# A fused attention and mixture-of-experts block: weight splits spread over two slots, one operation moved, and the last wait moved from GpSimd to SyncE

## The chip, the core and the metric

The program runs on one core of one Trainium2 chip. TensorE (PE in the profile, PEld for its weight loads), VectorE (DVE), ScalarE (ACT), GpSimd (POOL) and SyncE (SP) each run their own stream of instructions, in the order in which the program wrote it, and wait for each other on semaphores. The metric is the device time of one execution in microseconds, lower is better; the figure compared is the median of several runs.

## The reference

For 1024 tokens of 512 numbers the reference computes a layer norm and adds three things: the input, a grouped-query attention and a mixture of experts.

```
xn  = layernorm(x)                                  # (4, 256, 512)
q   = xn @ Wq ; k, v = split(xn @ Wkv)              # 32 heads of 16, 8 groups, causal, per sequence of 256
att = softmax(mask(q k') / 4) v @ Wo + bo
scores = sigmoid(xn @ gate_w') + bias               # 16 experts, the best 4 of each token
ffn = sum over chosen e of cw[e] * (silu(xn Wg[e]') * (xn Wu[e]')) @ Wd[e]'   +  a shared expert of the same form
out = x + att + ffn
```

## The kernel before

**Slots.** The token rows that choose an expert are gathered in groups of 128, called slots. There are 47 slots (NSLOT), sorted by expert, so an expert's slots stand next to each other. Which slot begins a new expert depends on the data; here, read from where the weight splits stand in the trace, these are the slots 1, 6, 11, 12, 13, 18, 19, 20, 21, 22, 26, 29, 30, 32 and 40 (the first expert's slot 0 is prepared earlier).

**Steps.** The main part of the program, from about 112 us to 480 us, is 48 steps, 12 for each of the 4 sequences (`b`). Step s does slot s of the experts, and beside it a part of the attention: the 8 head groups `g` of a sequence are spread over its 12 steps j by a table, so that a group has one or two steps.

```
BESIDE = ((0, 1), (2,), (3,), (4, 5), (6,), (7, 8), (9,), (10, 11))
```

In step s TensorE transposes the rows of slot s+1 (L1265), multiplies slot s by the gate and up weights (`slot_gate_up`, 12 matmuls on L1209 with `xgT`), transposes the gated values of slot s-1 (L1232), multiplies slot s-2 by the down weights (`slot_down`, 6 matmuls on L1209 with `zT`), and does the attention's scores for the maxima (`scores_for_max`, L1244 and L1249, which overwrite the banks that the exponential reads), the scores (L1331 to L1339) and the weighted sum (`weighted`, L1354). In two steps of a sequence it also multiplies by the output matrix (`project_out`, L1366).

**Split weights.** The products of the experts are made three times, with a high and a low part of each operand. When a slot begins a new expert, its weights are split: ScalarE copies the high part (`weights_high`, L632), then VectorE subtracts it from the raw weights to get the low part (`gu_low`, L1012, for gate and up; `down_low`, L1047, for down). The gate/up weights come in two halves of 1024 columns (HALVES), the down weights in one. The raw weights (`wraw`) and the split ones (`wsplit`) have two places each, used by experts in turn. SyncE loads raw weights in one fixed order; the load of expert e waits until both halves of expert e-2 are split (L379), and ScalarE waits for the load at L631.

In step s both halves of slot s+1's weights are split: on ScalarE between `x_high` (L628, the high part of the rows) and `tanh` (L609), on VectorE between `x_low` (L1007) and `gated` (L842, L847). `slot_gate_up` of the next step waits for both. The splits stand in an If on a register that is 0 when the slot begins no new expert.

**What stands behind the splits.** On ScalarE a step ends with `z_rows` (L622, L624), `y_evac` (L658, the result of `slot_down`), `context_evac` (L715, first step of a sequence), `high16` (L711, the 16-bit high part of the exponentials) and the down split; the next step of a new group begins with the exponential (`numerators`, L705). On VectorE the step has `x_low`, `context` (L1071, L1072, L1076: the weighted sums divided by their denominators), the splits, `maxima` (L997, twice), `gated`, `z_rest` (L989), the down split, `attention_out` (L1086) and `low16` (L1065, which needs `high16`). In the first step of a group of two, `context` is left to the second, where it stands ahead of the splits and of `gated`. TensorE's `weighted` of one group waits for `context` of the group before (its sums, `csum_done`).

**End.** GpSimd gathers rows, adds each slot's result into the output by an indirect DMA (L506), and adds the attention's rows by a DMA (L513). After its last issue it waits for `att_out`, that is until the last of these has landed (L541), and then leaves its stream. SyncE has nothing to do after the last weight load. All engines meet in the barrier that ends the block (L93).

## Time and profile before

| what | value |
|---|---|
| median of 3 runs | 502.7 us (502.25 to 503.31) |
| profiled execution, its own time | 504.71 us |
| its span, first to last instruction | 502.9 us |
| PE busy | 454.6 us, 90% of the span |
| VectorE busy | 360.7 us, 72% |
| ScalarE busy | 284.4 us, 57% |
| GpSimd busy | 192.5 us, 38% |

Busy times are sums over the span; an engine that is 90% busy sets the pace in most stages, but what a change is worth is read from the waits of the stage that it touches.

### The profile page before, as it was taken

To read this page: it belongs to the slowest core of one execution; us is meant where nothing else is said; L and a number is where in the kernel's file an instruction comes from. 1 tells how busy PE (TensorE), PEld (TensorE's weight loads), DVE (VectorE), ACT (ScalarE), POOL (GpSimd) and SP (SyncE) were. 2 spreads that over 40 slices of the span, in tenths; PEclk is the share of its full clock that TensorE was granted. 3 is DMA by queue.
4 is the path that set the end of the run, shared out by engine and by line. 5 is a ranking of instruction groups with operands and counts; after the bars stand their busy time and mean duration, and the time that the engine had idled before them with its cause. 6 is when DMAs were issued, how large, how long until landed. Compare 5 with 4: busy or idle time off the path is not lost.

```text
span 502.9 us, 9687 instructions
## 1 busy us (share of the span) xinstructions
PE 454.6 (90%) x3074; PEld 348.6 (69%) x3074; DVE 360.7 (72%) x624; ACT 284.4 (57%) x435; POOL 192.5 (38%) x159
## 2 busy tenths in 40 slices
PE   5997999967998998999897999998999999999870
PEld 5776888845786786767675776686777857777630
DVE  7588874776787779849889887389789638775610
ACT  2732332504766776837787756486866637676510
POOL 2111649512444453324344444242344433353221
PEclk9998999988999998999999999998999999999995
DMA  6925853849947545886597778658864434443333
GB/s 254 410 64 144 182 197 90 290 158 216 273 119 174 121 73 145 227 266 117 92 293 201 246 184 139 193 116 180 239 133 87 85 66 73 76 85 46 49 55 42
DMA packets 31877, 77.92 MB, mean 155 GB/s; under 512 B 4048, under 2 KB 11728, under 8 KB 28912
## 3 DMA queue, kind: packets, MB, share of 16 engines
q0 software_dynamic: 11856, 27.27, 29.4%
q1 hardware_dynamic: 18864, 45.92, 28.7%
q10 hardware_dynamic: 1104, 4.06, 4.0%
q8 instruction: 28, 0.46, 0.4%
q14 instruction: 25, 0.20, 0.1%
HBM read 54.04 MB, written 23.07 MB: 153 GB/s over the span
## 4 chain that ended last, share of the span: by engine, by line
PE 59%; DMA 16%; DVE 10%; issue 5%; ACT 5%; ACTq 1%; DVEq 1%; POOL 1%; SPq 0%; POOLq 0%
PE psum L1209 34%; DMA out<-ysb,tab 8%; DMA out<-third_out,tab 4%; PE psum L1366 3%; PE psum L1172 3%; PE psum L1244 3%; PE psum L1354 3%; DMA xn_rows<-xn 2%; PE psum L1265 2%; PE psum L1249 2%; PE psum L1331 2%; PE psum L1232 2%; DVE wsplit L1012 2%; ACT wsplit L632 2%; DVE negm L997 1%
## 5 line engine op out<-in xcount | busy, mean ns | idle before, releaser
L1209 PE MATMUL psum<-wsplit,xgT 128*128 (+1 forms) x660 | 173.8, 415 | 11.1 <-DVE wsplit L1012 11.0
L1209 PEld LDWEIGHTS psum<-wsplit,xgT 128*128 128x128 f32 x660 | 126.0, 197 | 38.2 <-issue 12.9
L506 POOL DMA_INDIRECT out<-ysb,tab x32 | 55.5, 1734 | 127.1 <-ACT ysb L658 56.9
L1209 PE MATMUL psum<-wsplit,zT 128*128 (+1 forms) x330 | 92.7, 417 | 3.7 <-DVE zT L983 3.5
L1209 PEld LDWEIGHTS psum<-wsplit,zT 128*128 128x128 f32 x330 | 59.7, 192 | 16.8 <-issue 6.1
L997 DVE TENSOR_REDUCE negm<-psum 128x4 f32<-128x512 f32 x64 | 59.4, 954 | 12.6 <-PE psum L1249 12.2
L1065 DVE TENSOR_TENSOR plo<-xn,phi 128x1536 f16<-128x1536 f32 x32 | 56.2, 1756 | 11.1 <-ACT phi L711 10.1
L705 ACT ACTIVATE xn<-psum 128x1536 f32<-128x1536 f32 x32 | 46.3, 1448 | 22.4 <-PE psum L1339 14.0
L1007 DVE TENSOR_TENSOR xgT<-psum,xgT 128x512 fp32r<-128x512 f32 x47 | 32.3, 688 | 36.8 <-ACT xgT L628 36.0
L632 ACT ACTIVATE wsplit<-wraw (+1 forms) x48 | 48.9, 1054 | 5.8 <-SPq L376 5.8
L496 POOL DMA_INDIRECT xg<-xn_rows,tab x32 | 38.7, 1211 | 34.7 <-PE psum L1265 19.0
L506 POOL DMA_INDIRECT out<-third_out,tab x15 | 27.9, 1858 | 59.2 <-ACT third_out L658 24.9
L609 ACT ACTIVATE th<-psum 128x256 f32<-128x256 f32 x55 | 21.1, 384 | 46.2 <-PE psum L1209 46.0
L711 ACT ACTIVATE phi<-xn 128x1536 f16<-128x1536 f32 x32 | 47.2, 1475 | 0.0
L1012 DVE TENSOR_TENSOR wsplit<-wraw,wsplit (+1 forms) x32 | 37.8, 1221 | 7.7 <-ACT wsplit L632 5.5
L658 ACT ACTIVATE ysb<-psum,tab 128x512 f32<-128x512 f32 x32 | 21.9, 684 | 24.8 <-PE psum L1209 23.0
L628 ACT ACTIVATE xgT<-psum 128x512 fp32r<-128x512 f32 x47 | 27.9, 593 | 8.1 <-issue 8.1
L842 DVE SCALAR_TENSOR_TENSOR zh<-th,psum 128x256 f32<-128x256 f32 x55 | 22.8, 414 | 10.6 <-ACT th L609 7.9
L1366 PE MATMUL psum<-wo_sb,stage 128*128 128x512 f32 x64 | 28.9, 596 | 0.4 <-DVE xn L1086 0.4
L1172 PE MATMUL psum<-xT,wqk_sb 128*128 128x256 f32 x128 | 29.0, 380 | 0.0
L1354 PEld LDWEIGHTS psum<-v_pack,phi 128*128 128x128 f16 x384 | 20.8, 96 | 10.2 <-issue 7.8
L1172 PEld LDWEIGHTS psum<-xT,wqk_sb 128*128 128x128 f32 x128 | 24.2, 190 | 3.9 <-issue 0.5
(192 smaller groups left out, 728.4 us busy)
## 6 DMA issues: line engine op xcount, KB each, us to landing
wraw<-wexp SPq DMA_DIRECT2D x17, 1024.0 KB, 6.8
wraw<-wexp SPq DMA_DIRECT2D x17, 512.0 KB, 4.5
q_parts<-stage SPq DMA_DIRECT2D x16, 192.0 KB
xn<-x SPq DMA_DIRECT2D x4, 512.0 KB, 5.3
xn_rows<-xn SPq DMA_DIRECT2D x8, 256.0 KB, 9.7
ctxs<-x SPq DMA_DIRECT2D x8, 256.0 KB, 4.7
out<-ysb SPq DMA_DIRECT2D x8, 256.0 KB, 3.3
out<-xn POOLq DMA_DIRECT2D x8, 256.0 KB, 4.2
```

The lines of the kernel that those rows point to most:

```text
L496: nc.gpsimd.indirect_dma_start(out=rows_in[s % 3], out_offset=None, in_=xn_rows, in_offset=rows_of(s)).then_inc(xg_in[s % 3], 16)
L506: nc.gpsimd.indirect_dma_start(out=out, out_offset=rows_of(s), in_=rows_out[s % 3], in_offset=None, compute_op=ALU.add).then_inc(y_out[par ...
L632: S(wsplit[:, place, 0, cols], wraw[:, place, cols], ACT.Copy).then_inc(w_high[part], 1)
L705: S(pexp[:, g % 2, :], psum[:, 0:3, :].rearrange("p a n -> p (a n)"), ACT.Exp, scale=SCALE).then_inc(exp_done, 1)
L711: S(phi[:, g % 2, :], pexp[:, g % 2, :], ACT.Copy).then_inc(hi16_done, 1)
L997: V.tensor_reduce(negm[:, g // 4, 0, REP * (g % 4):REP * (g % 4) + REP, qt], s_, AX.X, ALU.max, negate=True).then_inc(negm_done, 1)
L1012: V.tensor_tensor(wsplit[:, place, 1, HALVES[half]], wraw[:, place, HALVES[half]], wsplit[:, place, 0, HALVES[half]].bitcast(F32), ALU.sub ...
L1065: V.tensor_tensor(plo[:, g % 2, :], pexp[:, g % 2, :], phi[:, g % 2, :], ALU.subtract).then_inc(lo16_done, 1)
L1172: last = MM(psum[:, dst, i * T:(i + 1) * T], wqk_sb[:, k, f * P:(f + 1) * P], xT[:, k, T * b:T * (b + 1)], start=k == 0, stop=k == KD - 1, ...
L1209: last = MM(dst, lhs(a, k), split_weights(place, w, c), start=m == 0, stop=m == len(products) - 1)
L1354: last = MM(psum[:, PV, c:c + VCOL], p_[:, g % 2, col:col + P], v_pack[:, QT * (g % B) + kt, 2 * b + g // B, 0:VCOL], start=m == 0, stop=m ...
L1366: last = MM(bank(to), ctxT[:, qt, k, :], wo_sb[:, k, :], start=k == 0, stop=k == KD - 1)
```

## The change

Three edits. First, the gate/up split of a new expert is cut in two: in step s the first half for slot s+2 and the second half for slot s+1. The first half stands, on ScalarE, behind `y_evac` and ahead of the second `context_evac` and of `high16`, and on VectorE at the very end of the step. Ahead of step 0, the first half for slot 1 is split. Second, the `context` that stood behind `x_low` now stands behind `gated`. Third, GpSimd's last wait is gone, and SyncE waits at its end for all result DMAs.

```diff
@@ sync
             announce(1, NE - 1)
+            for par in range(2):
+                newest = NSLOT - 1 - (NSLOT - 1 - par) % 2
+                sp.wait_ge(y_out[par], 16 + 16 * (newest // 2 + 1))
+            sp.wait_ge(att_out, 16 * QT * B + 16)
@@ gpsimd
                 sequence(b, b == B - 1)
-            pool.wait_ge(att_out, 16 * QT * B + 16)
@@ scalar
-            def gate_up_high(number):
+            def gate_up_high(number, half):
 
                 with act.If(number > 0):
-                    place = bass.ds((number + 1) % 2, 1)
-                    weights_high(place, number, HALVES[0], 0)
-                    weights_high(place, number, HALVES[1], 0)
+                    weights_high(bass.ds((number + 1) % 2, 1), number, HALVES[half], 0)
                 act.end_ifs()
...
                         if s + 1 < NSLOT:
-                            gate_up_high(number)
+                            gate_up_high(number, 1)
                         if s < NSLOT:
                             tanh(NT + s, par)
...
                         if s >= 2 and not down_first:
                             y_evac(s - 2)
+                        if s + 2 < NSLOT:
+                            gate_up_high(ahead[1], 0)
                         if b and j == 0:
                             context_evac(b - 1, 1, PV)
...
             ahead = None, first_in(1)
+            gate_up_high(ahead[1], 0)
@@ vector
                         if b and j == 2:
                             attention_out(b - 1, 1, PV)
-                        if not first and g:
-                            context(b, g - 1)
...
                         if s + 1 < NSLOT:
-                            gate_up_low(number)
+                            gate_up_low(number, 1)
...
                         if s < NSLOT:
                             gated(NT + s, j % 2)
+                        if not first and g:
+                            context(b, g - 1)
                         if s:
                             z_rest(s - 1)
...
                             low16(b, g)
+                        if s + 2 < NSLOT:
+                            gate_up_low(ahead[2], 0)
...
             ahead = None, None, first_in(1)
+            gate_up_low(ahead[2], 0)
```

ScalarE, end of step 9 and start of step 10 (the first step of the last group of sequence 0): `y_evac` (L658), `high16` (L711), the If of the down split (L648), `numerators` (L705), `x_high` (L628). Before:

```order
L658 ACTIVATE ysb<-psum,tab 128x512 [waits y_out0,dn_ps]
L711 ACTIVATE phi<-xn 128x1536 [waits pv_ps,exp_done]
L648 COMPARE_AND_BRANCH
L632 ISA [waits down_ready]
L632 ISA
L632 ACTIVATE wsplit<-wraw 128x1024
L648 UNCONDITIONAL_BRANCH
L705 ACTIVATE xn<-psum 128x1536 [waits lo16_done,st_ps]
L628 ACTIVATE xgT<-psum 128x512 [waits xt_ps]
```

The same place in the changed program, where all line numbers are 1 to 3 higher:

```order
L659 ACTIVATE ysb<-psum,tab 128x512 [waits y_out0,dn_ps]
L643 COMPARE_AND_BRANCH
L635 ISA [waits gu_ready]
L635 ISA
L635 ACTIVATE wsplit<-wraw 128x1024
L643 UNCONDITIONAL_BRANCH
L712 ACTIVATE phi<-xn 128x1536 [waits pv_ps,exp_done]
L649 COMPARE_AND_BRANCH
L635 ISA [waits down_ready]
L635 ISA
L635 ACTIVATE wsplit<-wraw 128x1024
L649 UNCONDITIONAL_BRANCH
```

A split that waits for a load (`gu_ready`) now stands between `y_evac` and `high16`; the pair between `x_high` and `tanh` has become a single one (not shown).

VectorE, from `low16` (L1065) of step 10 into step 11, the second step of that group: `x_low` (L1007), `context` (L1071 to L1076), the If with the splits (L1058, L1012), `gated` (L842, L847). Before:

```order
L1065 TENSOR_TENSOR plo<-xn,phi 128x1536 [waits hi16_done]
L1007 TENSOR_TENSOR xgT<-psum,xgT 128x512 [waits xt_high]
L1071 RECIPROCAL den<-psum 128x8 [waits pv_ps]
L1072 TENSOR_REDUCE csum<-psum 128x128
L1076 TENSOR_TENSOR ctxs<-csum,den 128x2x64 [waits csum_done,dve_step]
L1058 COMPARE_AND_BRANCH [waits ctx_done]
...
L1012 TENSOR_TENSOR wsplit<-wraw,wsplit 128x1024
...
L1012 TENSOR_TENSOR wsplit<-wraw,wsplit 128x1024
L1058 UNCONDITIONAL_BRANCH
L842 SCALAR_TENSOR_TENSOR zh<-th,psum 128x256 [waits z_done,th_done]
L847 SCALAR_TENSOR_TENSOR zz<-zh,psum 128x256 [waits zt_ps,dve_step]
```

The same place in the changed program:

```order
L1068 TENSOR_TENSOR plo<-xn,phi 128x1536 [waits hi16_done]
L1062 COMPARE_AND_BRANCH
...
L1016 TENSOR_TENSOR wsplit<-wraw,wsplit 128x1024
L1062 UNCONDITIONAL_BRANCH
L1011 TENSOR_TENSOR xgT<-psum,xgT 128x512 [waits xt_high]
L1062 COMPARE_AND_BRANCH
...
L1016 TENSOR_TENSOR wsplit<-wraw,wsplit 128x1024
L1062 UNCONDITIONAL_BRANCH
L846 SCALAR_TENSOR_TENSOR zh<-th,psum 128x256 [waits z_done,th_done]
L851 SCALAR_TENSOR_TENSOR zz<-zh,psum 128x256 [waits zt_ps,dve_step]
L1074 RECIPROCAL den<-psum 128x8 [waits pv_ps]
L1075 TENSOR_REDUCE csum<-psum 128x128
```

Of the two splits one now stands ahead of `x_low`; `context` stands behind both and behind `gated`.

## Rows read from the trace of the kernel before

**Rows 1.** The page: span, and busy time of TensorE with its share and instructions.
```profile
span 502.9 us, 9687 instructions
PE 454.6 (90%) x3074; PEld 348.6 (69%) x3074; DVE 360.7 (72%) x624; ACT 284.4 (57%) x435; POOL 192.5 (38%) x159
```
**Rows 2.** Waits of TensorE, 112 to 480 us: us in total, times, longest.
```profile
PE psum L1209 <- DVE wsplit L1012: 11.0, 6, 3.2
```
**Rows 3.** Timeline, gate/up products: start, us, instruction, in brackets idle before and releaser.
```profile
120.91 4.60 PE L1209 MATMUL psum<-wsplit,xgT 128*128 x12 [2.37 <-DVE wsplit L1012]
127.00 3.01 PE L1209 MATMUL psum<-wsplit,xgT 128*128 x12
...
193.27 4.62 PE L1209 MATMUL psum<-wsplit,xgT 128*128 x12 [2.01 <-DVE wsplit L1012]
...
275.18 4.60 PE L1209 MATMUL psum<-wsplit,xgT 128*128 x12 [3.23 <-DVE wsplit L1012]
```
**Rows 4.** Windows: stretch, us, busy us of each engine, PEclk (granted clock), DMA share, GB/s.
```profile
194.00:196.80 2.80, 2.80 (x8) 2.15 (x8) 2.70 (x5) 1.97 (x3) 0.71 (x1) 0.50 1.05 226
```
**Rows 5.** Instructions of the block's end (L93): duration min/median/max in ns, first and last start.
```profile
L93 SPq DRAIN  x1: 13/13/13, 373.6 to 373.6; - x1
...
L93 POOLq COMPARE_BRANCH  x1: 41/41/41, 496.5 to 496.5; - x1
L93 POOLq DRAIN  x1: 5944/5944/5944, 496.7 to 496.7; - x1
```
**Rows 6.** Timeline, GpSimd's last two issues.
```profile
490.64 1.88 POOL L513 DMA_DIRECT2D out<-xn  x2 [3.82 <-DMA out<-ysb,tab]
```
**Rows 7.** The page's costliest groups: operation, count, busy us, mean ns, idle before, releaser.
```profile
L632 ACT ACTIVATE wsplit<-wraw (+1 forms) x48 | 48.9, 1054 | 5.8 <-SPq L376 5.8
L1012 DVE TENSOR_TENSOR wsplit<-wraw,wsplit (+1 forms) x32 | 37.8, 1221 | 7.7 <-ACT wsplit L632 5.5
...
L842 DVE SCALAR_TENSOR_TENSOR zh<-th,psum 128x256 f32<-128x256 f32 x55 | 22.8, 414 | 10.6 <-ACT th L609 7.9
```
**Rows 8.** Timeline of ScalarE, end of step 9.
```profile
183.10 1.47 ACT L711 ACTIVATE phi<-xn 128x1536 f16<-128x1536 f32 x1
```
**Rows 9.** Timeline of VectorE, steps 9 to 11.
```profile
184.68 1.76 DVE L1065 TENSOR_TENSOR plo<-xn,phi 128x1536 f16<-128x1536 f32 x1
...
188.08 1.88 DVE L997 TENSOR_REDUCE negm<-psum 128x4 f32<-128x512 f32 x2 [0.95 <-PE psum L1249]
...
196.68 0.51 DVE L1072 TENSOR_REDUCE csum<-psum 128x128 f32<-128x384 f32 x1
```
**Rows 10.** Timeline of TensorE, the down product of step 11.
```profile
197.86 1.64 PE L1209 MATMUL psum<-wsplit,zT 128*128 x6
```
**Rows 11.** Timeline of ScalarE, end of step 20 and step 21.
```profile
274.29 1.06 ACT L632 ACTIVATE wsplit<-wraw  x1 [3.27 <-SPq L376]
275.25 1.44 ACT L705 ACTIVATE xn<-psum 128x1536 f32<-128x1536 f32 x1
...
277.63 2.01 ACT L632 ACTIVATE wsplit<-wraw  x2 [0.46 <-SPq L376]
```
**Rows 12.** Timeline of TensorE, scores for the maxima in step 21, scores of step 22.
```profile
279.84 0.39 PE L1244 MATMUL psum<-k_pack,q_pack 96*128 96x128 bf16 x4
...
283.26 0.59 PE L1331 MATMUL psum<-xT,beside 98*128 98x512 bf16 x2
```
**Rows 13.** Timeline, step 24 and 25: VectorE's `low16`, and TensorE's second output product.
```profile
308.16 1.76 DVE L1065 TENSOR_TENSOR plo<-xn,phi 128x1536 f16<-128x1536 f32 x1 [2.07 <-ACT phi L711]
314.56 3.70 PE L1366 MATMUL psum<-wo_sb,stage 128*128 128x512 f32 x8 [0.35 <-DVE xn L1086]
```
**Rows 14.** Timeline, step 35: TensorE's down product, and VectorE's sums of `context`.
```profile
389.40 1.64 PE L1209 MATMUL psum<-wsplit,zT 128*128 x6
390.30 0.50 DVE L1072 TENSOR_REDUCE csum<-psum 128x128 f32<-128x384 f32 x1
```
**Rows 15.** Timeline of TensorE, scores of step 40.
```profile
427.69 0.59 PE L1331 MATMUL psum<-xT,beside 98*128 98x512 bf16 x2 [1.23 <-DVE negm L997]
```

More of the change, by code:

```diff
@@ L1054, in down_low_of, with gate_up_low @@
                 dve.end_ifs()
-            def gate_up_low(number):
+            def gate_up_low(number, half):
                 with dve.If(number > 0):
-                    gu_low(bass.ds((number + 1) % 2, 1), number, 0)
-                    gu_low(bass.ds((number + 1) % 2, 1), number, 1)
+                    gu_low(bass.ds((number + 1) % 2, 1), number, half)
                 dve.end_ifs()
```

## The prediction

> **What bounds the kernel now.** I read the page first, then TensorE's waits in the steps, then the timeline around each of them, and last the block's end. TensorE is busy 454.6 of 502.9 us [rows 1], so in the steps it is the engine to follow: work on the others counts only where TensorE, or the end, waits for it. The chain of waits on the page names indirect DMAs from 250 to 306 us, but that is a false lead: `y_evac` of slot 22 needs the buffer of slot 19, free long before, and is really ended by its product. The waits that the change can touch are the six of `slot_gate_up` on VectorE's low part, 11.0 us together, the longest 3.2 [rows 2]. They cost more than their idle time: behind the waits of 2.37, 2.01 and 3.23 us the twelve matmuls take 4.6 us, where an undisturbed slot takes 3.01 [rows 3], and there the granted clock is 0.50 [rows 4], that is 1.2 GHz; idle stretches of TensorE of about 2 us or more came before it. A fourth, at slot 29, is like these. A wait of 1.23 us cost no clock [rows 15]. So each of the four long waits takes some 1.6 us more than it shows.
>
> The end is a second place. GpSimd's last issue is done at 490.64 + 1.88 = 492.5 [rows 6]. It then waits for the landing until 496.5, and only then starts a DRAIN of 5.94 us, from 496.7 to 502.6 [rows 5]; nothing else runs by then.
>
> **The change part by part.** *The end.* With the wait on SyncE, whose own drain took 13 ns [rows 5], GpSimd branches and drains at once: from about 492.7 to 498.6, while the last DMAs land (496.5). If the drain keeps its length, the end comes 496.5 - 492.5 = **4.0 us earlier**. The other bound is 0, if the drain lasts until some 6 us after the landing whenever it begins. I take 4.0: SyncE's row says that a drain need not cost anything by itself, so the 5.94 us are something that GpSimd does, and at 496.7 nothing of its own was left to wait for, all its DMAs having landed.
> The Trainium skill ("VectorE: DVE Perf Modes", The DRAIN you can't avoid) says that the boilerplate drains at a program's start and end take about 12 ns on all five engines. By it moving the wait would give nothing; SyncE's 13 ns agree, GpSimd's 5,944 ns do not, and here the row decides. The skill's "GPSIMD Engine Reference" (Instruction dispatch) puts the first call of freshly loaded code at about 6 us (5.95 measured); if the drain is such a load, the sum would be the 4.0 above. No run here shows what the drain does.
>
> *The halves.* The work stays the same: 1.05 us on ScalarE and 1.22 on VectorE for each half [rows 7], 15 experts. One VectorE pass less now stands ahead of the product. That would take 1.2 us off each wait, were nothing else to move. But the early half stands on ScalarE behind `y_evac`, which waits for TensorE at the end of its step, and ahead of `high16`, so `high16` and all behind it come a full copy later.
>
> Slot 11: `high16` began at 183.10 and took 1.47 [rows 8]; now it ends at 183.10 + 1.05 + 1.47 - 0.1 = 185.5. VectorE's `low16`, which began at 184.68, begins 0.9 later, and the early half (1.1 net of overlap) stands behind it: 2.0 later, of which the 0.95 idle ahead of `maxima` absorbs one [rows 9]. `maxima` stand ahead of the late half, which so begins 1.1 later and is 1.1 shorter: **0 gained**. Slot 29 has the same order: 0.
>
> Step 11, last of its group: `weighted` needs the sums of `context`, which ended at 196.68 + 0.51 = 197.2 [rows 9], 2.3 ahead of the down product's end at 197.86 + 1.64 = 199.5 [rows 10]. Now an early half, a late half and `gated` stand ahead of them: 2 x 1.22 + 0.9 [rows 7] = 3.3, so they end at 200.4 to 200.5. TensorE, which went on at once, stands for **1.1**.
> Step 35, without splits: the sums ended at 390.30 + 0.50 = 390.8, the down product at 389.40 + 1.64 = 391.0 [rows 14]. With `gated` in front (0.9) they end at 391.7: **0.8**. Step 23 has the same form; there TensorE waits for a DMA right behind, and I put it at half: **0.4**. Steps j = 5 and 8, where `context` moves too, have a whole step to spare.
>
> Slots 20 to 22: here loads are late. ScalarE already waited until 274.29 for down weights and until 277.63 for the gate/up weights of slot 22 [rows 11]. The early half of slot 22 now stands at the end of step 20, and waits there for this same load, which cannot come sooner: its place in SyncE's order, behind a down load that waits for VectorE, is unchanged. Behind the waiting copy are the down split and the exponential of step 21. That starts at 277.6 + 2 x 1.05 - 0.2 = 279.5 instead of 275.25 [rows 11] and ends at 280.9, while `scores_for_max`, which needs it, ran at 279.84 [rows 12]: slot 21's wait of 3.23 goes, and one of over 3 comes a little later on the same engine. From the exponential's start to the late half were 277.63 - 275.25 - 0.46 = 1.9 us; then its copy (1.05), VectorE's pass (0.4 of latency and 1.22) and `maxima` (1.88 [rows 9]) end at 285.9. The scores that wait for them stood at 283.26 [rows 12]: **2.6 lost**.
>
> Step 25 (split for slot 26): VectorE waited 2.07 us for `high16`, and everything up to `attention_out` follows without a gap; TensorE already waited 0.35 us for that [rows 13]. One copy earlier on ScalarE, so **1.1 lost**.
>
> Slot 1: its early half stands ahead of step 0, where ScalarE comes late, so the first exponential is 1.25 us later. The late half ends about where the pair did (0.1 lost), but the 2.37 us in one piece become two pieces of about 1.5 with matmuls between. Without the slow clock 1.6 are gained, with it 0. The nearer row is 1.23 without [rows 15], not 2.01 with [rows 3]: I take **1.6 gained**.
> Slots 6, 18, 32 and 40, worked the same way, lie between 0.25 gained and 0.25 lost, together 0.2 gained; at slots 6 and 18 what TensorE waits for becomes the DMA of the maxima, issued behind the later `high16`. Slots 12, 13, 19 and 30 have cover of 1 us or more. The 47 added branches on each engine are hidden behind the operation dispatched before them; without that cover they would cost under 0.1 us each.
>
> Sum for the steps: 1.1 + 0.8 + 0.4 + 2.6 + 1.1 + 0.1 - 0.2 - 1.6 = 4.3 lost; at the end 4.0 gained. That is 0.3 us more than the profiled execution's 504.71, which lies 2.0 above the median of the runs, as its clock starts and stops outside the span and with the profiler on. On the median: 502.7 + 0.3 = **503.0 us**.
>
> **The rivals.** *The drain moves nothing* (the slower side): it lasts until some 6 us after the last landing, whoever waits. Decided by one thing, whether it still ends near 502.6 when begun at 492.7. For it: idle drains are short [rows 5], so this one may be waiting. Price: the 4.0 not gained, 503.0 + 4.0 = 507.0 us. *No new waits in the steps*: what the six waits lose and the new ones take cancel within 1 us, since idle time of ScalarE and VectorE takes up more than I allow. Then the end alone counts: 502.7 - 4.0 = 498.7. Against it: at slots 11 and 26 the rows leave no idle time to take up [rows 9, 13]. *The waits go as meant*: each of the six is shorter by one pass of 1.22 or all it had (0.95, 0.47), 6.3 us in all, with the end 502.7 - 10.3 = 492.4; half the four clock losses on top would make 489. Against it is the order on ScalarE. *The late load costs more*: the wait on ScalarE in step 20 and the two waits at steps 11 and 25 each bring the slow clock, some 1.6 each where VectorE does not cover it: 503.0 + 3 = 506.
>
> **How the numbers follow.** Changes within 0.2%, 501.7 to 503.7, are about what a measurement of this kernel cannot tell from none. My forecast has 0.42, with its own range of 501 to 504.7 (slot 1's clock back, or a gain of the same size): 0.10 of it lies below 501.7, 0.20 within, 0.12 above. The drain that moves nothing has 0.22, all slower. No new waits has 0.18 and the waits gone 0.06, both faster. The late load has 0.12: 0.08 slower, 0.04 the same. Together 0.34 faster, 0.24 the same, 0.42 slower. The range reaches from 498.0 (no new waits, with a little over) to 507.8 (the unmoved drain, with a little over); outside are the waits gone and the tails of these two, under 0.2.
>
> **What would show it.** GpSimd's DRAIN starts some 4 us ahead of the last landing and lasts about 6 us. TensorE's wait on VectorE's split falls from 11.0 to about 5 us, with slots 11 and 29 still in it and slot 21 nearly gone. Its wait on the sums of `context` at the end of steps 11, 23 and 35 grows, by over 2 us together. ScalarE's wait for loads, 5.8 us before [rows 7], becomes 9 or more with one of about 6 in step 20, and TensorE then waits for the exponential in step 21. The last step's products end 4 us later than before. I am wrong in the steps if the last product ends no later, wrong at the end if the drain does not begin early or does not end early, and wrong about slot 1 if its product still takes 4.6 us.

## The result and the profile after

The changed kernel takes 509.7 us (median of 4 runs, 507.43 to 512.17) against 502.99 us before: the ratio is 1.0138, with a 95% interval of 1.0104 to 1.0172. It is slower, by far more than the prediction's 503.0, and lies above its range, which ended at 507.8. Ratios here and below leave out the few slow executions, those over 1.5% above the fastest of their kernel, and so need not be the quotient of the medians, which are of all executions.

The page of its profiled execution (508.65 us), to set beside [rows 1]:

```profile
span 506.9 us, 9821 instructions
PE 450.1 (89%) x3074; PEld 344.4 (68%) x3074; DVE 359.9 (71%) x624; ACT 284.7 (56%) x435; POOL 191.8 (38%) x159
```

TensorE has the same work and is 4.5 us less busy, since some products regained the full clock; yet the span is 4.0 us longer, so it must wait 8.5 us more. TensorE's waits in the steps (us in total, times, longest), the view of [rows 2], show for whom:

```profile
PE psum L1360 <- DVE csum L1075: 5.4, 3, 3.1
PE psum L1337 <- DMA q_pack<-negmT: 4.4, 2, 2.4
PE psum L1215 <- DVE wsplit L1016: 3.9, 4, 1.3
PE psum L1250 <- ACT xn L706: 3.8, 2, 2.4
PE psum L1271 <- DVE xgT L1011: 2.0, 3, 1.1
```

The wait on the split fell from 11.0 us to 3.9, a gain of 7.1. In its place stand waits for the sums of `context` (`csum`), for a DMA from ScalarE (`q_pack<-negmT`) and for the exponential (`xn`). The DMA carries the maxima of the next four groups, which the first scores with them need. The waits one by one, in TensorE's timeline, with the products that answer to [rows 3]:

```profile
119.93 3.02 PE L1215 MATMUL psum<-wsplit,xgT 128*128 x12 [1.30 <-DVE wsplit L1016]
...
153.46 0.59 PE L1337 MATMUL psum<-q_pack,k_pack 98*128 98x512 bf16 x2 [1.93 <-DMA q_pack<-negmT]
...
154.90 4.58 PE L1215 MATMUL psum<-wsplit,xgT 128*128 x12
...
192.95 3.02 PE L1215 MATMUL psum<-wsplit,xgT 128*128 x12 [0.98 <-DVE wsplit L1016]
...
200.71 0.18 PE L1360 MATMUL psum<-v_pack,phi 128*128 128x49 bf16 x1 [3.14 <-DVE csum L1075]
...
274.78 3.02 PE L1215 MATMUL psum<-wsplit,xgT 128*128 x12 [0.56 <-DVE wsplit L1016]
...
280.44 0.40 PE L1250 MATMUL psum<-k_pack,q_pack 96*128 96x128 bf16 x4 [2.42 <-ACT xn L706]
...
317.86 3.70 PE L1372 MATMUL psum<-wo_sb,stage 128*128 128x512 f32 x8 [1.30 <-DVE xn L1089]
...
346.79 3.04 PE L1215 MATMUL psum<-wsplit,xgT 128*128 x12 [1.02 <-DVE wsplit L1016]
...
353.86 0.59 PE L1337 MATMUL psum<-q_pack,k_pack 98*128 98x512 bf16 x2 [2.44 <-DMA q_pack<-negmT]
```

Slots 1, 11, 21 and 29 wait less and their products take 3.02 to 3.04 us, at the full clock. But slot 6 has a slow product now, 4.58 us without any wait of its own, right behind the wait of 1.93 us for the DMA. The windows view of its middle (stretch, us, busy of each engine, then the granted clock, 0.52) shows 1.2 GHz, as in [rows 4]:

```profile
155.50:158.50 3.00, 3.00 (x9) 2.33 (x8) 1.06 (x2) 1.18 (x2) 1.13 (x1) 0.52 0.94 300
```

The end: the instructions of the block's end, as in [rows 5] (duration in ns, start in us).

```profile
L93 POOLq DRAIN  x1: 10050/10050/10050, 496.6 to 496.6; - x1
L93 SPq COMPARE_BRANCH  x1: 38/38/38, 502.4 to 502.4; - x1
```

The drain does begin early, 5.7 us ahead of the last landing at 502.34 and while GpSimd is still issuing that DMA. But it now lasts 10.05 us: it ends at 506.68, 4.34 us behind that landing, where before it ended 502.63 - 496.50 = 6.1 behind. The end gained 1.8 us, not 4.0.

Where the profiled execution lost its time, read from the starts of the slots' first gate/up matmuls in both traces (the listed steps; the others changed by -0.1 together):

| steps | before, us | after, us | difference | predicted |
|---|---|---|---|---|
| 0 and 1 | 13.63 | 12.78 | -0.85 | -1.5 |
| 5 and 6 | 15.45 | 17.18 | +1.73 | about 0 |
| 10 and 11 | 17.02 | 18.51 | +1.49 | +1.1 |
| 17 and 18 | 15.86 | 16.10 | +0.24 | about 0 |
| 20 to 22 | 26.60 | 26.80 | +0.20 | +2.6 |
| 23 | 7.54 | 8.17 | +0.63 | +0.4 |
| 25 | 13.37 | 14.31 | +0.94 | +1.1 |
| 28 and 29 | 16.35 | 17.24 | +0.89 | 0 |
| 35 | 6.55 | 7.35 | +0.80 | +0.8 |
| 39 to 41 | 21.78 | 22.09 | +0.31 | about 0 |
| slots 0 to 46 | 352.61 | 358.87 | +6.26 | +4.3 |

This execution was one of the faster ones of the changed kernel: its 508.65 us lie 3.9 above the profiled one of before, the medians 6.7 apart. The granted clock, a mean over the whole execution, was 0.979 in it and 0.964 in that of before, so the two traces are not equal draws. The other traces below tell which rows of this table come again.

### The profile page after: what moved, and what is told of

It reads as the page before. It is cut to its first block, busy times and chain, and to the rows that moved or that the text cites. A ratio compares the mean times of both kernels' runs of the same rounds, so it can differ in the third digit from the quotient of the medians.

```text
span 506.9 us, 9821 instructions
## 1 busy us (share of the span) xinstructions
PE 450.1 (89%) x3074; PEld 344.4 (68%) x3074; DVE 359.9 (71%) x624; ACT 284.7 (56%) x435; POOL 191.8 (38%) x159
## 4 chain that ended last, share of the span: by engine, by line
PE 54%; DMA 19%; DVE 8%; ACT 7%; issue 6%; ACTq 1%; DVEq 1%; POOL 0%; SPq 0%; POOLq 0%
PE psum L1215 27%; DMA out<-ysb,tab 8%; PE psum L1250 4%; PE psum L1178 3%; PE psum L1372 3%; DMA out<-third_out,tab 3%; PE psum L1360 3%; PE psum L1255 2%; ACT phi L712 2%; PE psum L1271 2%; DMA q_pack<-negmT 2%; ACT wsplit L635 2%; PE psum L1337 2%; DMA out<-xn 2%; DMA wraw<-wexp 2%
## 5 line engine op out<-in xcount | busy, mean ns | idle before, releaser
L1215 PE MATMUL psum<-wsplit,xgT 128*128 (+1 forms) x660 | 167.4, 403 | 3.9 <-DVE wsplit L1016 3.9
L1215 PEld LDWEIGHTS psum<-wsplit,xgT 128*128 128x128 f32 x660 | 121.3, 190 | 28.7 <-issue 5.2
L635 ACT ACTIVATE wsplit<-wraw (+1 forms) x48 | 50.2, 1052 | 15.9 <-issue 8.5
L500 POOL DMA_INDIRECT xg<-xn_rows,tab x32 | 36.5, 1140 | 34.1 <-PE psum L1271 18.8
L1016 DVE TENSOR_TENSOR wsplit<-wraw,wsplit (+1 forms) x32 | 39.0, 1219 | 9.7 <-ACT wsplit L635 6.5
L1360 PE MATMUL psum<-v_pack,phi 128*128 128x49 bf16 x384 | 23.9, 184 | 7.3 <-DVE csum L1075 7.3
```

What stands on the lines that cost most here:

```text
L500: nc.gpsimd.indirect_dma_start(out=rows_in[s % 3], out_offset=None, in_=xn_rows, in_offset=rows_of(s)).then_inc(xg_in[s % 3], 16)
L635: S(wsplit[:, place, 0, cols], wraw[:, place, cols], ACT.Copy).then_inc(w_high[part], 1)
L1016: V.tensor_tensor(wsplit[:, place, 1, HALVES[half]], wraw[:, place, HALVES[half]], wsplit[:, place, 0, HALVES[half]].bitcast(F32), ALU.sub ...
L1215: last = MM(dst, lhs(a, k), split_weights(place, w, c), start=m == 0, stop=m == len(products) - 1)
L1360: last = MM(psum[:, PV, c:c + VCOL], p_[:, g % 2, col:col + P], v_pack[:, QT * (g % B) + kt, 2 * b + g // B, 0:VCOL], start=m == 0, stop=m ...
```

## The experiments

Two sessions of four kernels each took the change apart; two more sessions tested the places that came out of them. "Before" is the kernel before, timed on the same chip in the same session. The differences below are of medians; the intervals are those of the ratio. Each kernel has one trace, taken of one execution.

| kernel | median, us | before, us | ratio, 95% interval |
|---|---|---|---|
| e1_end | 500.64 | 502.58 | 0.9982 (0.9958 to 1.0005) |
| e1_context | 503.46 | 502.58 | 1.0017 (0.9988 to 1.0045) |
| e1_halves | 509.54 | 502.58 | 1.0158 (1.0121 to 1.0195) |
| e1_no_end | 512.35 | 502.58 | 1.0193 (1.0147 to 1.0239) |
| e2_behind | 506.06 | 502.22 | 1.0067 (1.0037 to 1.0097) |
| e2_ahead | 503.57 | 502.22 | 1.0021 (0.9998 to 1.0043) |
| e2_context_5_8_end | 496.85 | 502.22 | 0.9883 (0.9841 to 0.9924) |
| e2_drain | 501.79 (1 run) | 502.22 | - |
| e3_context_11 | 505.28 | 503.61 | 1.0051 (1.0030 to 1.0073) |
| e3_slot22_old | 508.13 | 503.61 | 1.0109 (1.0076 to 1.0141) |
| e3_context58_ahead_end | 498.01 | 503.61 | 0.9897 (0.9866 to 0.9929) |
| e3_context58_slot1_end | 498.60 | 503.61 | 0.9905 (0.9867 to 0.9943) |
| e4_slots_6_18_30 | 506.83 | 503.14 | 1.0084 (1.0053 to 1.0114) |
| e4_slots_context | 503.03 | 503.14 | 0.9976 (0.9944 to 1.0007) |

**The three edits apart.** First the end alone (e1_end):

```diff
+            for par in range(2):
+                newest = NSLOT - 1 - (NSLOT - 1 - par) % 2
+                sp.wait_ge(y_out[par], 16 + 16 * (newest // 2 + 1))
+            sp.wait_ge(att_out, 16 * QT * B + 16)
...
-            pool.wait_ge(att_out, 16 * QT * B + 16)
```

> The end alone: GpSimd no longer waits for the last landing, SyncE does; all else as before. Theory A (the drain runs until a fixed time behind the last landing of GpSimd's DMAs, shorter when it is entered early; in the changed kernel it ended 4.3 us behind that landing, in the kernel before 6.1): 1.8 us faster, near 501.2, drain of about 10 us from 492.6. Theory B (the drain has a length of its own of 5.9 us, as the prediction took it): 4.0 us faster, 499. Theory C (the drain waits for the landing and takes the same 6 us behind it): no change, 503.

It is 1.9 us faster by the medians and 0.9 by the ratio, whose interval just includes none; so the time alone does not decide. Its end, in the same view as above:

```profile
L93 POOLq DRAIN  x1: 9154/9154/9154, 487.2 to 487.2; - x1
```

The last landing was at 492.05 and the drain ended at 496.38, 4.34 behind, while theory B asked for 5.9 from the drain's start and theory C for 6 from the landing: theory A. The number is the same, to 0.01 us, in all kernels here whose GpSimd has no last wait and no work behind its last DMA; with the wait it is 6.14 in every one.

The context alone (e1_context), with both halves of a split in their old place:

```diff
-                        if not first and g:
-                            context(b, g - 1)
...
                         if s < NSLOT:
                             gated(NT + s, j % 2)
+                        if not first and g:
+                            context(b, g - 1)
```

> The context behind gated alone, both halves of a split in their old place. Theory A (the move delays the sums that the weighted product of the next group waits for, whatever the halves do): 1 us at step 11, 0.8 at step 35, 0.4 at step 23, 505 in all, and the wait on the sums of context rises from 2.3 to over 4 us. Theory B (the wait of 3.1 us at step 11 comes from the late high16 and the early halves, and the context only adds to it): within 1 us of the kernel before, no wait of over 1 us at step 11.

The time did not change measurably (+0.9 us), which speaks for B, but the waits speak for A: TensorE's waits in the steps are

```profile
PE psum L1354 <- DVE csum L1072: 6.7, 4, 2.5
PE psum L1209 <- DVE wsplit L1012: 6.6, 4, 2.0
```

the wait on the sums is 6.7 us (2.0 of it at the last step, as before), 2.5 of it at step 11:

```profile
198.28 0.20 PE L1354 MATMUL psum<-v_pack,phi 128*128 128x49 bf16 x1 [2.48 <-DVE csum L1072]
```

The wait on the split fell from 11.0 to 6.6. Gains and losses in different steps nearly cancel. Neither theory had the gain, so the next session took the edit apart by steps.

The halves alone (e1_halves), that is the diff of the change for `gate_up_high` and `gate_up_low` without the rest; and halves with context, without the end (e1_no_end).

> The halves over two steps alone, context and end as before. Theory A (the early half stands ahead of high16 and makes it and everything behind it late): slower by 4 to 6 us, 507 to 509; waits for the DMA of the maxima at steps 6 and 30 of about 2 us, a wait for the exponential in step 21 of over 2 us, slot 6 at the slow clock. Theory B (the loss of the changed kernel is mostly the moved context): within 1.5 us of 503.

> Halves and context as in the changed kernel, the end as before. Theory A (the end gives back about 1.8 us): 511 to 512, slower than the changed kernel by 1.8. Theory B (the end gave nothing or cost something): 509.7 or less. If halves and context simply add up, its difference to the kernel before is the sum of those of the two runs of them alone; if they make each other worse at step 11, it is about 2 us more.

The halves alone cost 7.0 us, all that the whole change costs. With the context it is 9.8, and the changed kernel's 6.7 lie 3 below that, which the intervals allow to be the 1.8 of the end. So the halves are the loss; the context adds to it, though in time that is clear only from the later runs, and the end gives a little back.

**Which engine's place costs.** Two kernels are e1_halves with ScalarE's early half moved: behind `high16` (e2_behind), or up between `z_rows` and `y_evac` (e2_ahead). VectorE's half stays.

```diff
# e2_behind
-                        if s + 2 < NSLOT:
-                            gate_up_high(ahead[1], 0)
...
                         if j == BESIDE[g][0]:
                             high16(b, g)
+                        if s + 2 < NSLOT:
+                            gate_up_high(ahead[1], 0)
# e2_ahead
                         if s:
                             z_rows(s - 1)
+                        if s + 2 < NSLOT:
+                            gate_up_high(ahead[1], 0)
                         if b and j == 0:
                             context_evac(b - 1, 0, PV)
                         if s >= 2 and not down_first:
                             y_evac(s - 2)
-                        if s + 2 < NSLOT:
-                            gate_up_high(ahead[1], 0)
```

> The halves alone as in the kernel with the halves alone (7.0 us slower than before), but ScalarE's early half stands behind high16 instead of ahead of it. Theory A (the loss is high16, and what follows from it: low16, the DMA of the maxima, attention_out): the waits for the DMA of the maxima at steps 6 and 30 fall from 5.0 us together to about 1, slot 6 keeps the full clock, step 25 loses nothing; 503 to 505. Theory B (the loss is VectorE's early pass at the end of the step, which delays x_low and maxima): 508 or more, the waits unchanged.

> The halves alone, with ScalarE's early half between tanh and z_rows, ahead of y_evac. Theory A (ScalarE's order is what costs; ahead of y_evac ScalarE has idle time, 24 us over 32 steps, that takes up part of the copy): high16 late by some 0.4 us instead of 1.05, 505 to 507. Theory B (VectorE's early pass costs): 509 as with the halves alone.

(As the diff shows, e2_ahead's half stands behind `z_rows` and ahead of `y_evac`, not ahead of `z_rows` as its expectation says.) Moving one copy of 1.05 us on ScalarE takes the loss from 7.0 us to 1.4 in e2_ahead, whose interval just includes none, better than theory A asked; VectorE's pass was left where it was, so theory B falls. e2_behind gave back only about half: slot 6 and step 25 were as before, but its waits for the DMA of the maxima did not fall (4.5 us): that was wrong. The reason is in the order on ScalarE, here the changed kernel at the end of step 4 and the start of step 5:

```profile
146.02 0.69 ACT L659 ACTIVATE third_out<-psum,tab 128x512 f32<-128x512 f32 x1 [1.27 <-PE psum L1215]
146.61 1.05 ACT L635 ACTIVATE wsplit<-wraw  x1
147.56 1.47 ACT L712 ACTIVATE phi<-xn 128x1536 f16<-128x1536 f32 x1
148.93 0.26 ACT L665 ACTIVATE negmT<-psum 64x128 bf16<-64x128 f32 x1
149.22 1.05 ACTq L667 DMA_DIRECT2D q_pack<-negmT  x1
```

`y_evac` waits 1.27 us for TensorE, then follow without a gap the early half for slot 6, `high16`, the copy of the maxima and the issue of their DMA. Behind `high16` the early half is still ahead of that DMA. In e2_ahead the same stretch reads:

```profile
143.42 1.06 ACT L632 ACTIVATE wsplit<-wraw  x1
144.73 0.69 ACT L656 ACTIVATE third_out<-psum,tab 128x512 f32<-128x512 f32 x1 [0.25 <-PE psum L1212]
145.31 1.47 ACT L709 ACTIVATE phi<-xn 128x1536 f16<-128x1536 f32 x1
146.69 0.26 ACT L662 ACTIVATE negmT<-psum 64x128 bf16<-64x128 f32 x1
146.98 1.05 ACTq L664 DMA_DIRECT2D q_pack<-negmT  x1
```

The copy lies in the idle time ahead of `y_evac`, of which 0.25 us is even left, and the DMA is issued 2.25 us behind the start of `y_evac` instead of 3.20. TensorE then waits 0.23 us for it, where the changed kernel waited 1.93:

```profile
150.46 0.59 PE L1334 MATMUL psum<-q_pack,k_pack 98*128 98x512 bf16 x2 [0.23 <-DMA q_pack<-negmT]
```

**The DMA of the maxima and the sums of context.** e4_slots_6_18_30 is the changed kernel with the old split for the slots whose early half stands in a step j = 4, so just ahead of that DMA:

```diff
                         if s + 1 < NSLOT:
+                            if s % SPS == 5:
+                                gate_up_high(number, 0)
                             gate_up_high(number, 1)
...
-                        if s + 2 < NSLOT:
+                        if s + 2 < NSLOT and s % SPS != 4:
                             gate_up_high(ahead[1], 0)
```

and the same on VectorE. e4_slots_context also puts the context of the steps j = 11 back:

```diff
+                        if j == 11:
+                            context(b, g - 1)
                         with_maxima = first and not (last and g >= 4)
...
                             gated(NT + s, j % 2)
-                        if not first and g:
+                        if j in (5, 8):
                             context(b, g - 1)
```

> The changed kernel, except that for the slots 6, 18 and 30 both halves are split in the step ahead of them, as before (for slot 42 too, which begins no expert): no early half stands ahead of the high16 behind which the DMA of the maxima is issued. Theory A (that DMA is what was missed: waits of 1.9 us at step 6 and 2.4 at step 30, with a slow clock behind the first, and up to 1.3 us at slot 18): these waits fall below 1 us, steps 5 and 6 take 15.4 us or less together instead of 17.2; 505 to 507. Theory B (the early half of slot 6 costs nothing that its absence gives back, since slot 6's own wait on the split returns): 509 to 510.

> The same, and the context of the steps j = 11 back in its place ahead of the splits. Theory A (the two mechanisms together, the DMA of the maxima and the sums of context at j = 11, are the loss of the changed kernel; with both gone only the end's 1.8 us gain, slot 1's gain, and the losses at steps 21 and 25 are left): 501 to 503. Theory B (the early halves cost in other ways too): 505 or more.

The ratio falls from 1.0138 for the changed kernel to 1.0084 and then to 0.9976; in medians the difference to before goes from +6.7 to +3.7 and -0.1 us. The first of them still waits for the sums (2.0 of it at the last step, which every kernel has and which lay behind the stretch shown of the changed kernel) but hardly for the DMA:

```profile
PE psum L1364 <- DVE csum L1077: 7.3, 4, 3.1
...
PE psum L1341 <- DMA q_pack<-negmT: 1.3, 2, 0.8
```

Steps 5 and 6 took 14.55 us together there, slot 6 at the full clock. By the times theory A holds for the first and, at the edge of its range, for the second: these two places make up most of the loss. The intervals of the changed kernel and of the first overlap a little (from 1.0104, to 1.0114), so its 3.0 us are less sure than what the context gave back.

The traces say less than the times about the DMA itself. At step 29 the early half's absence did not help in this one:

```profile
341.21 4.61 PE L1219 MATMUL psum<-wsplit,xgT 128*128 x12 [1.02 <-DVE wsplit L1018]
...
348.24 0.59 PE L1341 MATMUL psum<-q_pack,k_pack 98*128 98x512 bf16 x2 [0.81 <-DMA q_pack<-negmT]
```

The wait is short because slot 29 ran at the slow clock and TensorE came 1.6 us later; from the slot's start to the product that the DMA feeds it is 7.03 us, against 353.86 - 346.79 = 7.07 in the changed kernel. And e3_slot22_old (below), with the order of the changed kernel on ScalarE in step 4, again issues the DMA 3.20 us behind the start of `y_evac`, and yet TensorE hardly waits for it at step 5 (ScalarE's timeline, then TensorE's):

```profile
147.98 1.05 ACTq L667 DMA_DIRECT2D q_pack<-negmT  x1
```

```profile
150.46 0.59 PE L1341 MATMUL psum<-q_pack,k_pack 98*128 98x512 bf16 x2 [0.17 <-DMA q_pack<-negmT]
...
152.65 3.03 PE L1219 MATMUL psum<-wsplit,xgT 128*128 x12 [0.51 <-DVE wsplit L1018]
```

From the issue to that product it is 2.48 us here and 153.46 - 149.22 = 4.24 in the changed kernel. So the later issue takes the slack away, about 1 us, and how long the DMA then takes in an execution decides what is waited; steps 5 and 6 lost 1.7 to 2.1 us in three traces with this order and nothing in the fourth (14.61 us). What sets the DMA's time no run shows.

What is left of the loss, some 1.7 us without the end's gain, would fit steps 21 and 25 less slot 1's gain; no run tells that apart.

**The context at j = 11 alone** (e3_context_11), otherwise the kernel before:

```diff
-                        if not first and g:
+                        if j in (5, 8):
                             context(b, g - 1)
...
                             gated(NT + s, j % 2)
+                        if j == 11:
+                            context(b, g - 1)
```

> Only the context of the steps j = 11 stands behind gated; j = 5 and 8, splits and end as before. Theory A (the weighted product of the next group waits for these sums: in the kernel with the context alone steps 11, 23 and 35 grew by 2.4, 0.7 and 0.8): 3 to 4 us slower than before, 505.5 to 506.5, the wait on the sums of context 5 us or more. Theory B (given back on the way to the next step's wait): within 1 us of before.

It is slower by 1.7 us (2.6 by the ratio), less than expected: at step 11 the wait is 0.88 us, at steps 23 and 35 it is 1.64 and 0.70.

```profile
191.01 4.62 PE L1211 MATMUL psum<-wsplit,xgT 128*128 x12 [2.02 <-DVE wsplit L1012]
...
198.13 0.18 PE L1356 MATMUL psum<-v_pack,phi 128*128 128x49 bf16 x1 [0.88 <-DVE csum L1072]
```

How long step 11 waits for the sums depends on slot 11's product. Here it took 4.62 us; in e1_context, also without the halves, it took 3.03, TensorE came 1.6 us sooner, and the wait was 2.48. In the changed kernel it is 3.14, and in e1_halves, with the context in its old place, 1.23. So the moved context alone delays the sums, and the halves delay them some more. VectorE in the changed kernel there:

```profile
196.28 1.22 DVE L1016 TENSOR_TENSOR wsplit<-wraw,wsplit  x1
197.42 0.68 DVE L1011 TENSOR_TENSOR xgT<-psum,xgT 128x512 fp32r<-128x512 f32 x1
198.02 1.22 DVE L1016 TENSOR_TENSOR wsplit<-wraw,wsplit  x1
199.15 0.41 DVE L846 SCALAR_TENSOR_TENSOR zh<-th,psum 128x256 f32<-128x256 f32 x1
199.60 0.42 DVE L851 SCALAR_TENSOR_TENSOR zz<-zh,psum 128x256 f32<-128x256 f32 x1
199.94 0.20 DVE L1074 RECIPROCAL den<-psum 128x8 f32<-128x8 f32 x1
200.05 0.50 DVE L1075 TENSOR_REDUCE csum<-psum 128x128 f32<-128x384 f32 x1
```

The sums end at 200.55, and TensorE, which had regained its clock at slot 11 and was done with the down product at 195.94 + 1.63 = 197.57, stands until 200.71.

**The late load** (e3_slot22_old): the changed kernel with both halves of slot 22 in step 21 as before (conditions `s != 20` and `s == 21` in the two places of the diff of e4_slots_6_18_30).

> The changed kernel, except that both halves for slot 22, the one whose load is late, are split in step 21 as before. Theory A (the early half waits for a load that cannot come sooner, and holds the exponential of step 21; the term of 2.6 in the prediction): 2 to 3 us faster than the changed kernel, 507; steps 20 to 22 26.6 us together as before, where the changed kernel took 26.8, since slot 21's wait and slow clock come back only in part. Theory B (what it costs at step 21 it gives back at slot 21: the three steps took 26.6 us before and 26.8 after): no difference, 509 to 510.

508.13 us, ratio 1.0109 against 1.0138: the intervals overlap, so the time alone leaves it open. Steps 20 to 22 took 25.58 us against 26.80 in the changed kernel and 26.60 before, but single traces scatter as widely there: 25.92 and 27.03 in e1_end and e2_drain, whose steps are those of before, and 24.98 in e4_slots_6_18_30, which has the early half of slot 22. What the late load costs stays open. The wait itself is as foreseen; ScalarE's timeline of the changed kernel, beside [rows 11]:

```profile
277.05 2.00 ACT L635 ACTIVATE wsplit<-wraw  x2 [4.72 <-SPq L376]
278.96 1.43 ACT L706 ACTIVATE xn<-psum 128x1536 f32<-128x1536 f32 x1
```

The copy of the early half waits 4.72 us for the load, and the exponential behind it starts at 278.96, which gives TensorE's wait of 2.42 us at 280.44.

**The end of GpSimd's stream** (e2_drain): e1_end with three fills ahead of the drain.

```diff
                 sequence(b, b == B - 1)
+            nc.gpsimd.memset(plo[:, 0, :], 0.0)
+            nc.gpsimd.memset(plo[:, 1, :], 0.0)
+            nc.gpsimd.memset(phi[:, 0, :], 0.0)
```

> The end alone, with three fills of some 1.3 us each on GpSimd between its last issue and the end of its stream, so that the drain begins about 1 us ahead of the last landing instead of 4.8. Theory A (the drain lasts at least 5.94 us of its own, and ends no sooner than 4.34 behind the landing): it ends about 5 us behind the landing. Theory B (it ends 4.34 us behind the landing whenever it is entered ahead of it): 4.34. Theory C (entered early it costs its own time and then something per outstanding DMA): other than both.

The last of the fills in GpSimd's timeline, and the drain:

```profile
492.39 1.38 POOL L547 MEMSET phi<- 128x1536 f16 x1
```

```profile
L93 POOLq DRAIN  x1: 11336/11336/11336, 488.4 to 488.4; - x1
```

It ends at 499.72: 5.76 us behind the landing (493.96), so not B; and 499.72 - (492.39 + 1.38) = 5.95 us behind the last fill, the same 5.94 as in [rows 5]. Theory A, with the start counted from the end of GpSimd's own work.

**Toward a faster kernel.** The end, and the context moved only at j = 5 and 8, with whole splits (e2_context_5_8_end, the diffs of e1_end and of the `j in (5, 8)` above); the same with the halves as in e2_ahead (e3_context58_ahead_end); the same with only slot 1's early half ahead of step 0 (e3_context58_slot1_end).

> The end as in the changed kernel and the context behind gated only in the steps j = 5 and 8 of a sequence, not in j = 11; the splits as before. Theory A (in the kernel with the context alone the moved context shortened steps 5, 17, 20 and 29 by 0.9, 0.9, 2.2 and 1.5 us, since the split and gated come earlier, and cost 2.4, 0.7 and 0.8 at the steps j = 11): 3 to 5 us faster than the kernel with the end alone (500.6), 496 to 498. Theory B (these gains are chance of one profiled execution): 500 to 501.

> The end as in the changed kernel, context behind gated at j = 5 and 8 only, and the halves over two steps with ScalarE's early half ahead of z_rows. Theory A (the halves help where high16 is not late: slots 1 and 11): up to 2 us faster than with context and end alone (496.85). Theory B (the halves cost 1.3 us there too, as in the kernel with the halves ahead of z_rows, 503.6 against 502.2): 498.

> The end, the context at j = 5 and 8, and of the halves only the one of slot 1 ahead of step 0; all other splits whole and as before. Theory A (that half takes slot 1's wait and slow clock away and touches nothing else; steps 0 and 1 were 0.85 us shorter together in the changed kernel): 496.0. Theory B (slot 1's gain is lost again in the later waits): 496.9.

The first is the fastest kernel of the study, 1.2% faster than before. In its profile the product of slot 21 waits 1.52 us instead of 3.23 and keeps the full clock, and step 5 is 0.9 us shorter: in step 20 (j = 8) and step 5 `context` had stood ahead of the split and of `gated`. The other two are as fast within their intervals: the halves add nothing to it that can be measured. For the last one that speaks for its theory B: in its trace steps 0 and 1 are 2.1 us shorter than in the first kernel's, but begin 1.4 us later.

## Why the prediction was wrong

**What held.** The early half behind `y_evac` and ahead of `high16` as the source of the loss; shorter waits at slots 1 and 21; ScalarE's wait for the load in step 20 (4.7 us, foreseen as about 6) and TensorE's wait for the exponential behind it; the waits for the sums of `context` at steps 11, 23 and 35 and for `attention_out` at step 25. The terms of steps 23, 25 and 35 (0.4, 1.1, 0.8) were measured as 0.63, 0.94 and 0.80. Those of steps 25 and 35 come again in each trace of e1_no_end, e3_slot22_old and e4_slots_6_18_30, which have the same order there, to 0.01 us; step 23 took 8.06 us in e2_drain with nothing changed, so its term is not told from scatter. Slot 1's clock came back, with a product of 3.02 to 3.07 us in all ten traces that have its early half; but e2_drain, without it, kept the clock as well.

**The step that failed: the DMA of the maxima.** The prediction saw that at slots 6 and 18 "what TensorE waits for becomes the DMA of the maxima, issued behind the later `high16`", and put all of it between 0.25 gained and lost; slot 30 was given "cover of 1 us or more", and slot 29 no change. It gave no row for the slack of this DMA, and no term for a slow clock behind it. Measured were waits of 1.93 us at step 5's end and 2.44 at step 29's. In the trace of before the product of slot 6 took 3.03 us behind a wait of 0.95 on the split:

```profile
156.69 3.03 PE L1209 MATMUL psum<-wsplit,xgT 128*128 x12 [0.95 <-DVE wsplit L1012]
```

Now the 1.93 us came ahead of it and it took 4.58: a loss of clock that had no term. Steps 5 and 6 alone lost 1.73 us in the profiled execution, and 1.9 to 2.1 in e1_no_end and e1_halves, where four traces with these steps as before show 15.44 to 15.47; undoing the early half at these slots gave 3 us by the medians. Two things limit this account: e3_slot22_old has the same order and lost nothing at steps 5 and 6, so what had no term is a risk and not a fixed cost; and at step 29 the traces show no gain from undoing it.

**The end: right in kind, a size off.** The 4.0 us rested on a drain of fixed length. Measured, it takes 5.94 us of its own from the end of GpSimd's work but ends no sooner than 4.34 us behind the last landing, so the gain is 6.14 - 4.34 = 1.8 us. The rival by which it moves nothing fell as well.
The Trainium skill ("VectorE: DVE Perf Modes", The DRAIN you can't avoid) has boilerplate drains of about 12 ns on all five engines, from a program's preamble and postamble; no run shows whether the drains of the block's end are of that kind. SyncE's took 13 ns there, GpSimd's 5.94 to 11.3 us, and the runs decide. The Trainium skill ("GPSIMD Engine Reference", Instruction dispatch) has about 6 us, 5.95 measured, for a first call of freshly loaded code, the length found behind the fills; no run shows that the drain is such a call.

**Two more sizes.** Step 11 was put at 1.1 with nothing gained at slot 11. That the slot itself begins no sooner was nearly right: its wait fell by 1.0 us, but a new wait of 0.67 us for the maxima took most of it, and step 10 became 0.2 us shorter. But its product won 1.6 us through the clock, TensorE came that much sooner to the late sums, and the wait of 3.14 us took it all: a net of 1.5 in steps 10 and 11. With slot 11 at the slow clock, in e3_context_11, step 11 grew by 1.0, about as predicted. For slots 20 to 22 the 2.6 us left out that slot 21 would give back its wait and its slow clock, [rows 3] against 3.02 us now; the net was 0.2 in this trace, inside the scatter of the others.

Two terms are each 0.1 above their own working (391.7 - 391.0 at step 35, 200.5 - 199.5 at step 11), which changes little. And the prediction laid the 2.0 us between the profiled execution and the median of before to the profiler and to the clock's start and stop; but the span lies 1.7 to 1.9 us under the time in every execution on record, so these 2.0 are scatter between executions.

In sum the steps lost 6.3 us in this execution (4.3 predicted) and the end gave 1.8 (4.0 predicted). With slot 0's product 1.1 us sooner and 0.7 us more between the start of slot 46's and the last landing this is the 4.0 us of the two spans. The rest of the 6.7 us lies in executions other than the profiled one. e1_no_end, with the same steps, shows a second: 361.55 us from slot 0 to slot 46, 2.7 more than the changed kernel's 358.87, with slow products at slots 12 and 18 too. That such slow products are what sets the longer executions apart is likely but not shown, since only one execution of a kernel has a trace. The granted clock, which is on record for every execution, speaks for it: of the four of the changed kernel the shortest, 507.43 us, had 0.980 and the longest, 512.17, had 0.966; and longer executions of the kernel before had the lower clock in three of the four sessions of experiments (correlations of -0.68 to -0.89), but not in the second (-0.05).

## What to carry to other kernels

A copy moved forward on an in-order engine costs its length to everything between the old and the new place, so look there first for DMA issues: a DMA that was just in time has no slack left for an execution in which it takes longer, and here the same copy placed in a wait that the engine had anyway was almost free. A wait that is shortened for the bottleneck engine is worth only what the next wait of that engine doesn't take back, so follow its timeline to the next two or three waits. A single trace is one draw: look whether a step's time comes again in another kernel with the same order before a cause is read from it. And test the parts of a change by place: the `context` moved won in the steps j = 5 and 8 and lost in j = 11, which the sum hid.

## What the runs showed of the hardware

GpSimd's drain at the block's end is no formality: it lasted 5.94 us behind a last wait (seven traces), ended 5.95 us after GpSimd's last work in e2_drain, and 4.34 us behind the landing of its last DMA in the other eight; SyncE's takes 13 ns. TensorE's takes 6.4 to 6.7 us, but its last products run almost until then: in the trace of before it ends at 487.51, they at 487.47.

A wait of TensorE of 2.01 us does not always cost the clock. Slot 11 has this wait in the kernel before, with a product of 4.62 us [rows 3], and in e1_context, in TensorE's timeline:

```profile
191.17 3.03 PE L1209 MATMUL psum<-wsplit,xgT 128*128 x12 [2.01 <-DVE wsplit L1012]
```

The same wait, and the full clock. So has slot 1 in e2_drain, with the wait that cost 1.6 us in the kernel before:

```profile
118.69 3.04 PE L1215 MATMUL psum<-wsplit,xgT 128*128 x12 [2.37 <-DVE wsplit L1018]
```

And slot 29's wait of 1.02 us came with 3.04 us in the changed kernel and with 4.61 in e4_slots_6_18_30, both shown above. So the prediction's 1.6 us for each long wait have to be read as a chance, not as a price.

Executions of one kernel differ more than the first runs showed: the kernel before took 498.75 to 506.37 us in 23 runs of the first session of experiments, where the three that the prediction had lay within 1.1 us. One trace is one draw from that.
